# GpSimd takes the plain LayerNorm normalisations, the ternary weights and an output bias from VectorE in a two-layer gated cross-attention kernel

## The chip, the cores and the metric

The kernel runs on one core of one Trainium2 chip. The time is that of one execution on the device, in microseconds, and lower is better. Engines are named as the profile names them: PE is TensorE (PEld its weight loads), DVE is VectorE, ACT is ScalarE, POOL is GpSimd, SP is SyncE. PSUM is the memory into which PE writes; SBUF is the working memory from which all engines read.

## What is computed

A residual stream `x` of two batches of 512 tokens and 128 channels passes through two layers. Each layer is a cross-attention and a feed-forward net, and each of them is added back through a tanh gate.

```python
# layer 0
x = x + tanh(g_xattn[0]) * (attention(ln(x), ctx) @ Wo + bo)       # 16 heads, 77 context rows
h = ln(x)
gate = silu(bitlinear(h, w_gate)); up = bitlinear(h, w_up)
x = x + tanh(g_ffn[0]) * bitlinear(gate * up, w_down)
# bitlinear: activations rounded to 8 bits per token, weights to -1, 0, 1
#   scale = 1 / clip(mean(|w|), 1e-5);     wq = clip(round(w * scale), -1, 1) / scale
#   scale = 127 / clip(max(|x|), 1e-5);    xq = clip(round(x * scale), -128, 127) / scale
# layer 1
a = ln(x) * ln1_g + ln1_b                     # then self-attention a1 (masked after the softmax) + GELU net
a = ln(a) * ln2_g + ln2_b                     # then cross-attention a2 on ctx + GELU net
x = x + gate * a
x = x + gate * (softmax router) * expert_7(ln(x))
```

`ln` subtracts the mean of a token's 128 channels and divides by the root of the variance plus 1e-5.

## The kernel before

Tokens lie on the 128 partitions: a batch `b` (0 or 1) is four tiles `t` of 128 tokens by 128 channels, so a tensor such as `xn[:, b, t, :]` is one 128x128 tile. Each engine has its own program, written out by hand in order, and the programs meet at semaphores. An engine works its program in that order: an instruction that waits holds all behind it on the same engine.

The stages, with the time that they take in the profile: loading, folding the layer-0 projections into one key matrix and the first LayerNorm (0 to 23 us); the layer-0 cross-attention, 16 units `i` (23 to 84 us); the quantised feed-forward net, eight token tiles `n` (84 to 115 us); the LayerNorms and first projections of self-attention a1 (115 to 140 us); a1's 32 heads (140 to 280 us); its output and GELU net `a1f` (280 to 320 us); the cross-attention a2, again 16 units (323 to 377 us); the GELU nets `a2f` and `f1` (377 to 420 us).

**A LayerNorm** is done for one batch in these steps. DVE takes statistics (`ln_stats`, four L1167 and four L1170) and writes `var` (L1175). POOL raises it to the power -0.5 (`power`, L842) into `rstd`. DVE normalises (`ln_norm`): for a plain site four `tensor_scalar` of one tile each, `(src - mean) * rstd`, into `xn` (L1182); for the sites with gain and bias (`ln1`, `ln2`) four instructions with the gain (L1187) and four with `rstd` and the bias (L1191) into `x1`. DVE waits for `rstd` before the first of either, and behind `ln_norm` waits until it is complete. Then PE transposes `xn` (L397), ACT copies the result to `xnT` (L918, L921), and PE goes on with matmuls. Sites are called after what they feed: `x`, `f0`, `ln1`, `a1`, `a1f`, `ln2`, `a2`, `a2f`, `f1`.

**A unit of cross-attention** (`cross`, for `l0` and `a2`): PE scores (L470), DVE row maxima `nmx` (L1248), ACT eight exponentials (L988), DVE reciprocal sums `rden` (L1253), POOL multiplies the 128x616 probabilities by them (L851), PE transposes them (L397), DVE copies the transposes out of PSUM (L1260), PE multiplies by the values (L490). PE's program for step `i` is scores of `i`, values of `i-3`, transposes of `i-2`. Other work hangs in this loop by its step: on DVE `ternary` at steps 6, 8 and 10 of `l0` (three instructions on a 128x512 matrix, L1234, L1236, L1238), the output bias at steps 9 and 11 (L1304), LayerNorm `f0` of batch 0 at steps 13 to 15, and in `a2` at steps 0 to 2 the two LayerNorms `ln2` and `a2` of batch 1, at steps 13 and 14 `a2f` of batch 0. POOL computes `rstd` of `f0` behind its multiplication 12, of `a2` behind 0, of `a2f` behind 12.

**The quantised net**, per tile `n`: PE two matmuls (L564), ACT silu (L1035), DVE product with the second matmul (L1402), DVE the largest magnitude (L1411), its clip (L1408), reciprocal (L1414) and times 127 (L1416), ACT multiply and round by adding a large constant (L1050), DVE clip to -128..127 (L1421, waits for ACT's rounding of tile `n-2`), ACT to bf16 (L1058), PE transposes (L585), DVE copy (L1429), PE matmul (L596). The input of the net is rounded the same way: `scale_x`, `round_x` on ACT, `clip_x` on DVE (L1358), `x_to_bf16` on ACT.

At the start, DVE's program is: context statistics, statistics of `x`, normalisation of `x` for both batches, then `ctxn` (L1387), which waits for `crstd` from POOL (L864), and then its share of the copies of the folded keys out of three PSUM banks (L1210, `fold("l0", 0)`), which PE's fold matmuls (L438) need free.

## Time and profile before

| | |
|---|---|
| Time before, median of 3 runs | 426.03 us (424.16 to 428.45) |
| The profiled execution's own time | 422.04 us |
| its span, first to last instruction | 420.3 us |
| PE busy | 344.0 us, 82% of the span, 2037 instructions |
| PEld busy | 235.8 us, 56% |
| DVE busy | 315.2 us, 75%, 748 instructions |
| ACT busy | 279.4 us, 66% |
| POOL busy | 107.6 us, 26%, 206 instructions |
| Chain that ended last | PE 43%, DVE 13%, issue 7%, ACT 7%, POOL 1% |

Busy time is the time in which an engine has an instruction in work. Matmuls are pipelined, so a busy PE need not be at its peak. The clock of PE is granted in two levels, 1.2 GHz (0.5 in the profile) and 2.4 GHz (1.0). The chain that ended last is followed back from the last instruction to what released each step; in this trace it reaches back to 120 us only.

### The profile page before, as it was taken

The numbers are of one execution on the slowest core, as the hardware profiler recorded it, in microseconds if no ns is written. First come the engines' busy times: TensorE is split into PE (matmuls) and PEld (weight loads), VectorE is DVE, ScalarE is ACT, GpSimd is POOL, SyncE is SP. The second block draws the span as 40 slices with busy tenths as digits, with TensorE's granted clock in tenths as the row PEclk, the third lists the DMA queues.
The fourth block names the chain that finished last, engine by engine and source line by source line (L and its number), as shares of the span: only waits on it lengthen the run. The fifth ranks groups of instructions, "written<-read, shape, count | busy, mean of one in ns | idle before, by whom it ended". The sixth has DMA issues, their size and how long they took to land.

```text
span 420.3 us, 6805 instructions
## 1 busy us (share of the span) xinstructions
PE 344.0 (82%) x2037; PEld 235.8 (56%) x2038; DVE 315.2 (75%) x748; ACT 279.4 (66%) x965; POOL 107.6 (26%) x206
## 2 busy tenths in 40 slices
PE   4978999726437888998989988978998799977796
PEld 4756877602312444555545545566676588864656
DVE  3656789688885688899899998975757876855515
ACT  4465888657413787888889888853825899855051
POOL 5311344300010122232222222232101444520100
PEclk9999999966558999999999999999999899999989
DMA  7920000000003653861790494000000000000001
GB/s 222 346 100 2 2 1 2 1 0 1 2 0 82 158 136 89 200 140 26 168 207 3 101 205 96 0 4 0 2 0 2 1 2 0 2 0 2 0 0 51
DMA packets 8860, 24.75 MB, mean 59 GB/s; under 512 B 2667, under 2 KB 2744, under 8 KB 8568
## 3 DMA queue, kind: packets, MB, share of 16 engines
q1 hardware_dynamic: 8824, 24.32, 22.9%
q8 instruction: 17, 0.28, 0.3%
q14 instruction: 19, 0.16, 0.1%
HBM read 7.00 MB, written 0.52 MB: 18 GB/s over the span
## 4 chain that ended last, share of the span: by engine, by line
PE 43%; DVE 13%; issue 7%; ACT 7%; POOL 1%; DVEq 0%
PE ps L397 9%; PE ps L537 5%; PE ps L521 5%; DVE nm L1513 4%; PE ps L615 4%; PE ps L667 4%; PE ps L490 4%; PE ps L630 4%; ACT pring L1111 3%; PE ps L470 3%; PE ps L438 2%; DVE arena L1485 2%; PE ps L701 2%; DVE xn L1182 1%; PE ps L683 1%
## 5 line engine op out<-in xcount | busy, mean ns | idle before, releaser
L1111 ACT ACTIVATE pring<-ps,nm 128x512 f32<-128x512 f32 x128 | 87.0, 688 | 12.7 <-DVE nm L1513 9.6
L988 ACT ACTIVATE arena<-ps,nmx 128x77 f32<-128x77 f32 x256 | 79.1, 344 | 14.1 <-DVE nmx L1248 13.6
L1513 DVE TENSOR_REDUCE nm<-ps 128x2 f32<-128x1024 f32 x64 | 78.0, 1220 | 6.1 <-PE ps L630 5.9
L875 POOL TENSOR_SCALAR_AFFINE_SELECT pring<-pring 128x128 f32<-128x128 f32 x128 | 38.8, 303 | 109.5 <-ACT pring L1111 109.5
L630 PE MATMUL ps<-Ks,Qs 128*128 128x512 f32 x128 | 52.6, 463 | 8.6 <-ACT pring L1111 6.2
L397 PEld LDWEIGHTS ps<-ident,pring 128*128 128x128 f32 x352 | 39.4, 140 | 32.7 <-issue 17.8
L397 PE MATMUL ps<-ident,pring 128*128 128x128 f32 x352 | 52.1, 277 | 6.7 <-ACT xn L1078 2.8
L988 ACT ACTIVATION_READ_ACCUMULATOR arena<-ps,nmx 128x1 f32 x256 | 57.3, 224 | 0.0
L851 POOL TENSOR_TENSOR arena<-arena,rden 128x616 f32<-128x616 f32 x32 | 39.2, 1226 | 63.1 <-DVE rden L1253 63.1
L490 PE MATMUL ps<-arena 128*128 128x128 f32 x320 | 42.4, 280 | 6.3 <-DVE arena L1260 6.3
L490 PEld LDWEIGHTS ps<-arena 128*128 128x128 f32 x320 | 38.6, 192 | 15.5 <-DVE arena L1260 14.9
L1485 DVE COPY arena<-ps 128x384 f32<-128x384 f32 x64 | 39.5, 617 | 7.7 <-PE ps L397 7.5
L842 POOL TENSOR_TENSOR rstd<-var,minus_half 128x4 f32<-128x4 f32 x18 | 18.2, 1010 | 105.3 <-DVE var L1175 105.2
L470 PE MATMUL ps<-arena,xnT 128*128 128x320 f32 x128 | 41.0, 445 | 3.3 <-ACT arena L988 1.7
L1260 DVE COPY arena<-ps 128x384 f32<-128x384 f32 x64 | 27.9, 477 | 10.4 <-PE ps L397 10.4
L630 PEld LDWEIGHTS ps<-Ks,Qs 128*128 128x128 f32 x128 | 21.3, 190 | 25.0 <-ACT pring L1111 14.1
L1248 DVE TENSOR_REDUCE nmx<-ps 128x8 f32<-128x616 f32 x32 | 25.5, 798 | 9.9 <-PE ps L470 9.6
L397 PE MATMUL ps<-ident,arena 128*128 128x128 f32 x200 | 29.3, 279 | 2.9 <-POOL arena L851 1.1
L470 PEld LDWEIGHTS ps<-arena,xnT 128*128 128x128 f32 x128 | 22.4, 195 | 10.1 <-ACT arena L988 2.7
L397 PEld LDWEIGHTS ps<-ident,arena 128*128 128x128 f32 x200 | 23.2, 143 | 5.5 <-issue 1.6
L1111 ACT ACTIVATION_READ_ACCUMULATOR pring<-ps,nm 128x1 f32 x128 | 25.8, 202 | 0.0
L1015 ACT ACTIVATE hid<-ps,cols_sb 128x512 f32<-128x512 f32 x24 | 16.1, 688 | 12.5 <-PE ps L521 12.4
(147 smaller groups left out, 539.4 us busy)
## 6 DMA issues: line engine op xcount, KB each, us to landing
Qs<-qh SPq DMA_DIRECT2D x24, 128.0 KB, 2.4
Qs<-ql SPq DMA_DIRECT2D x24, 128.0 KB, 2.4
Ks<-xo SPq DMA_DIRECT2D x24, 128.0 KB, 2.4
Ks<-xb SPq DMA_DIRECT2D x24, 128.0 KB, 2.4
wa_sb<-in_wa SPq DMA_DIRECT2D x1, 1536.0 KB, 15.2
early<-in_w SPq DMA_DIRECT2D x2, 512.0 KB, 8.2
wa_sb<-in_wa SPq DMA_DIRECT2D x1, 1024.0 KB, 17.4
Qs<-hid SPq DMA_DIRECT2D x16, 64.0 KB, 2.0
```

Of the source, the lines that this page charges most:

```text
L397: m = pe.transpose(bank(res)[0:width, t * parts:(t + 1) * parts], src(t), ident[0:parts, 0:parts])
L470: m = pe.matmul(bank(res)[:, 0:4 * HS], xnT[:, b, t * P:(t + 1) * P], FK[:, b, c0:c0 + 4 * HS], start=True, stop=True)
L490: m = pe.matmul(bank(res)[:, t * P:(t + 1) * P], PTc[:, j % 4, k, :], VO[:, b, half * (NCH // 2) + k, :], start=(half == 0 and k == 0), st ...
L630: filled(pe.matmul(bank(f"S{i}"), Qs[:, j, b, i * P:(i + 1) * P], Ks[:, j, b, :], start=True, stop=True), ("s1", n, i))
L851: pool.tensor_tensor(pv, pv, rden[:, j % 4, :].unsqueeze(2).to_broadcast([P, 8, M]), ALU.mult).then_inc(pn_ready, 1)
L875: pool.affine_select(out=blk, in_=blk, compare_op=ALU.is_gt, fill=0.0, base=0, pattern=[[1, P]], channel_multiplier=-1).then_inc(masked, 1)
L988: ins = act.activation(Pc[:, i % PC_SLOTS, h * HS:h * HS + M], bank(where[key])[:, h % 4 * HS:h % 4 * HS + M], ACT.Exp, bias=nmx[:, i % 4, ...
L1111: release(act.activation(pring[:, n % 2, i, :], bank(f"S{i}"), ACT.Exp, bias=nm1[:, n % 8, i:i + 1], accum_out=den1[:, n % 8, i:i + 1]), ( ...
L1248: dve.tensor_reduce(nmx[:, i % 4, :].rearrange("p (q h) -> p q h", q=2), src, AX.X, ALU.max, negate=True).then_inc(nmax_ready, 1)
L1260: release(dve.tensor_copy(PTc[:, j % 4, k0:k1, :].rearrange("p k n -> p (k n)"), bank(res)[:, 0:(k1 - k0) * P]), key)
L1485: release(dve.tensor_copy(dst, src), key)
L1513: dve.tensor_reduce(nm1[:, n % 8, 2 * u:2 * u + 2], pair(u), AX.X, ALU.max, negate=True).then_inc(nm1_ready, 1)
```

## The change

1. `normalise_tokens`, new, on POOL: behind `rstd` of each plain site POOL itself writes `xn`, four `tensor_scalar` of one 128x128 tile each. `ln_norm` is gone from DVE. `xn_ready` counts the plain sites alone.
2. `ternary` and the output bias move to POOL: one step behind each of its multiplications 1 to 12 of `l0`. The bias is now `bo * gate` once (128x128) and then one 128x512 addition per batch.
3. POOL's powers move inside `cross`: `f0` batch 0 from behind multiplication 12 to behind 13, `a2` batch 1 from 0 to 4. PE's transposes and ACT's copy of `a2` batch 1 move from step 3 to step 6.
4. The sites with gain and bias stay on DVE: `ln_gain` no longer waits for `rstd`, only `ln_bias` does. For `ln2` batch 1 they are spread over steps 0 to 3 of `a2` and its statistics go to step 4.
5. The clips of rounded activations (L1358, L1421) are left out: a value scaled by 127 over its token's largest magnitude rounds to at most 127. The constant 1/127 is folded into the clip of the maximum, so that the multiplication by 127 (L1354, L1416) goes too, and `dout` takes one instruction instead of two.
6. Before `a1f`, POOL also waits for `RT_ready` and `OT_ready`, since `xn` holds other data during the heads.

```diff
@@ gpsimd
+            def normalise_tokens(site, b):
+                src = {"x": r, "f0": r, "a1": x1, "a1f": xo, "a2": x1, "a2f": xo, "f1": r}[site]
+                pool.wait_ge(rstd_ready, nth(site, b))
+                for t in range(NT):
+                    ins = pool.tensor_scalar(xn[:, b, t, :], src[:, b, t, :], mv[:, b, t, 0:1],
+                                             rstd[:, b, t:t + 1], ALU.subtract, ALU.mult)
+                ins.then_inc(xn_ready, 1)
@@ power
                             .then_inc(rstd_ready, 1)
+                        if site not in LN_AFFINE:
+                            normalise_tokens(site, b)
@@ gpsimd cross
-                    if site == "l0" and j == 12:
+                    if site == "l0" and 1 <= j < 4:
+                        output_bias(j - 1)
+                    if site == "l0" and 4 <= j < 13:
+                        ternary((j - 4) // 3, (j - 4) % 3)
+                    if site == "l0" and j == 13:
                         power("f0", batches=[0])
-                    if site == "a2" and j == 0:
+                    if site == "a2" and j == 4:
                         power("a2", batches=[1])
@@ tensor cross
-                    if site == "a2" and i == 3:
+                    if site == "a2" and i == 6:
                         ln_transposes("a2", 1)
@@ vector
-            def ln_norm(site, b, src, affine=None, dst=None):
+            def ln_gain(site, b, src, tiles=range(NT)):
+                for t in tiles:
+                    did(dve.scalar_tensor_tensor(x1[:, b, t, :], src[:, b, t, :], mv[:, b, t, 0:1],
+                                                 row(site + "_g"), ALU.subtract, ALU.mult))
+
+            def ln_bias(site, b, tiles=range(NT)):
+                settle()
                 dve.wait_ge(rstd_ready, nth(site, b))
@@ vector, quantised net
                 if 1 <= n <= NB * NT:
-                    did(dve.reciprocal(hinv[:, bj, tj:tj + 1], hmx[:, bj, tj:tj + 1]))
-                    settle()
-                    dve.tensor_scalar(hinv[:, bj, tj:tj + 1], hinv[:, bj, tj:tj + 1], 127.0, None, ALU.mult)\
-                        .then_inc(hscale_ready, 1)
-                if 2 <= n < NB * NT + 2:
-                    j = n - 2
-                    dve.wait_ge(hround_ready, j + 1)
-                    dve.tensor_scalar(h_in[:, j % 4, :], h_in[:, j % 4, :], MAGIC + 127.0, MAGIC - 128.0,
-                                      ALU.min, ALU.max).then_inc(hclip_ready, 1)
+                    dve.reciprocal(hinv[:, bj, tj:tj + 1], hmx[:, bj, tj:tj + 1]).then_inc(hscale_ready, 1)
@@ vector
             ln_stats("a1", 0, x1)
             f0_out(1)
-            ln_norm("a1", 0, x1)
             ln_stats("ln1", 1, r)
```

POOL at the start of the program, in the kernel before (`crstd` is the factor of the context's LayerNorm, `arena` holds folded keys and their zero pads):

```order
L842 TENSOR_TENSOR rstd<-var,minus_half 128x4 [waits var_ready] x2
L864 TENSOR_TENSOR crstd<-cvar,minus_half 77x2 [waits cvar_ready]
L830 MEMSET arena 128x16x3 x4
L835 MEMSET arena 128x8x3 [waits full_T1]
L835 MEMSET arena 128x8x3 x2
```

The same place in the changed kernel:

```order
L889 TENSOR_TENSOR rstd<-var,minus_half 128x4 [waits var_ready]
L850 TENSOR_SCALAR xn<-r,mv,rstd 128x128 [waits rstd_ready]
L850 TENSOR_SCALAR xn<-r,mv,rstd 128x128 x3
L889 TENSOR_TENSOR rstd<-var,minus_half 128x4 [waits var_ready]
L850 TENSOR_SCALAR xn<-r,mv,rstd 128x128 [waits rstd_ready]
L850 TENSOR_SCALAR xn<-r,mv,rstd 128x128 x3
L917 TENSOR_TENSOR crstd<-cvar,minus_half 77x2 [waits cvar_ready]
L838 MEMSET arena 128x16x3 x4
```

Eight normalising instructions now stand ahead of `crstd` and of the zeroed pads.

DVE in the quantised net, one tile, in the kernel before (`hid` holds the products and their roundings, `hmx` and `hinv` the largest magnitude and its inverse):

```order
L1402 SCALAR_TENSOR_TENSOR hid<-ps,du,hid 128x512 [waits silu_ready,full_S3]
L1408 TENSOR_SCALAR hmx<-hmx 128x1
L1411 TENSOR_REDUCE hmx<-hid 128x1 [waits free_S3,dve_step]
L1414 RECIPROCAL hinv<-hmx 128x1
L1416 TENSOR_SCALAR hinv<-hinv 128x1 [waits dve_step]
L1421 TENSOR_SCALAR hid<-hid 128x512 [waits hround_ready]
L1429 COPY hid<-ps 128x512 [waits full_T0]
```

The same tile in the changed kernel:

```order
L1416 SCALAR_TENSOR_TENSOR hid<-ps,du,hid 128x512 [waits silu_ready,full_S3]
L1421 TENSOR_SCALAR hmx<-hmx 128x1 [waits dve_step]
L1425 TENSOR_REDUCE hmx<-hid 128x1 [waits free_S3,dve_step]
L1428 RECIPROCAL hinv<-hmx 128x1
L1435 COPY hid<-ps 128x512 [waits full_T0]
```

Two of seven instructions are gone, and with the clip the wait for ACT's rounding.

## Rows read from the trace of the kernel before

**Rows 1.** Busy time by stretch, all engines: length; PE, PEld, DVE, ACT, POOL; clock, DMA
```profile
78.00:110.00 32.00, 15.90 (x103) 9.23 (x103) 25.54 (x85) 20.86 (x43) 2.23 (x2) 0.70 0.00 1
140.00:280.00 140.00, 122.07 (x759) 71.12 (x758) 126.47 (x163) 118.64 (x309) 39.25 (x129) 1.00 0.50 113
```

**Rows 2.** Timeline of 12 to 19 us: start, length, engine, instruction, idle before
```profile
12.91 1.02 POOL L842 TENSOR_TENSOR rstd<-var,minus_half 128x4 f32<-128x4 f32 x1 [6.77 <-DVE var L1175]
15.31 0.78 POOL L864 TENSOR_TENSOR crstd<-cvar,minus_half 77x2 f32<-77x2 f32 x1
17.05 0.53 DVE L1210 TENSOR_SCALAR arena<-ps 128x154 f32<-128x154 f32 x2
18.68 0.55 DVE L1210 TENSOR_SCALAR arena<-ps 128x154 f32<-128x154 f32 x2 [1.10 <-PE ps L438]
```

**Rows 3.** Timeline in the first attention, POOL and PE
```profile
55.04 1.24 PE L470 MATMUL ps<-arena,xnT 128*128 128x320 f32 x4
55.27 1.22 POOL L851 TENSOR_TENSOR arena<-arena,rden 128x616 f32<-128x616 f32 x1 [1.50 <-DVE rden L1253]
...
57.80 1.24 PE L470 MATMUL ps<-arena,xnT 128*128 128x320 f32 x4
61.08 1.24 PE L470 MATMUL ps<-arena,xnT 128*128 128x320 f32 x4
```

**Rows 4.** Timeline of the quantised net: table load ahead of it, one tile on DVE
```profile
83.59 1.28 ACT L910 ACT_TABLE_LOAD   x1
...
98.60 0.74 DVE L1402 SCALAR_TENSOR_TENSOR hid<-ps,du,hid 128x512 f32<-128x512 f32 x1
...
100.05 0.15 DVE L1414 RECIPROCAL hinv<-hmx 128x1 f32<-128x1 f32 x1
100.31 0.42 DVE L1421 TENSOR_SCALAR hid<-hid 128x512 f32<-128x512 f32 x1
100.64 0.42 DVE L1429 COPY hid<-ps 128x512 bf16<-128x512 bf16 x1
100.97 0.74 DVE L1402 SCALAR_TENSOR_TENSOR hid<-ps,du,hid 128x512 f32<-128x512 f32 x1
```

**Rows 5.** Timeline of 114 to 133 us, first LayerNorms of layer 1
```profile
114.91 1.14 DVE L1187 SCALAR_TENSOR_TENSOR x<-r,mv,rows_sb 128x128 f32<-128x128 f32 x4 [0.76 <-POOL rstd L842]
...
121.66 1.09 PE L397 MATMUL ps<-ident,xn 128*128 128x128 f32 x4 [6.85 <-DVE xn L1182]
...
130.23 1.01 POOL L842 TENSOR_TENSOR rstd<-var,minus_half 128x4 f32<-128x4 f32 x1 [6.10 <-DVE var L1175]
...
132.63 1.11 DVE L1182 TENSOR_SCALAR xn<-x,mv,rstd 128x128 f32<-128x128 f32 x4
```

**Rows 6.** Groups of instructions on POOL, shapes apart: busy us, mean ns, idle
```profile
L875 POOL TENSOR_SCALAR_AFFINE_SELECT pring<-pring 128x128 f32<-128x128 f32 x128 | 38.8, 303 | 109.5 <-ACT pring L1111 109.5
L842 POOL TENSOR_TENSOR rstd<-var,minus_half 128x4 f32<-128x4 f32 x18 | 18.2, 1010 | 105.3 <-DVE var L1175 105.2
```

**Rows 7.** Timeline, DVE and POOL where both read SBUF
```profile
55.89 0.88 DVE L1234 TENSOR_SCALAR pring<-pring,winv 128x512 f32<-128x512 f32 x1
...
214.78 0.43 DVE L1493 COPY xn<-rd 128x512 f32<-128x512 f32 x1
214.87 0.49 POOL L875 TENSOR_SCALAR_AFFINE_SELECT pring<-pring 128x128 f32<-128x128 f32 x1 [0.63 <-ACT pring L1111]
```

**Rows 8.** Timeline in the second attention, from its start to steady state
```profile
327.86 0.80 DVE L1248 TENSOR_REDUCE nmx<-ps 128x8 f32<-128x616 f32 x1
...
333.68 0.80 DVE L1248 TENSOR_REDUCE nmx<-ps 128x8 f32<-128x616 f32 x1
...
359.80 1.23 POOL L851 TENSOR_TENSOR arena<-arena,rden 128x616 f32<-128x616 f32 x1 [1.53 <-DVE rden L1253]
...
362.43 0.71 PE L397 MATMUL ps<-ident,arena 128*128 128x128 f32 x5
```

**Rows 9.** Timeline at 380 us, LayerNorm before the second plain FFN
```profile
380.54 1.12 DVE L1182 TENSOR_SCALAR xn<-xo,mv,rstd 128x128 f32<-128x128 f32 x4 [1.12 <-POOL rstd L842]
```

More of the change, by code:

```diff
@@ L71 @@
             ("f1", 0), ("f1", 1)]
+LN_AFFINE = ("ln1", "ln2")
+LN_PLAIN = [(site, b) for site, b in LN_ORDER if site not in LN_AFFINE]
 LN_TRANSPOSED = [(site, b) for site, b in LN_ORDER if site not in ("f0", "ln1", "ln2")]
@@ L882, in _ @@
             zero_diag(1)
+            pool.wait_ge(RT_ready, NSTEP)
             power("a1f", batches=[0])
@@ L1227, in mean_weights @@
                 settle()
[L1228 to L1238 removed]
+                dve.reciprocal(winv[:, :], wmean[:, :]).then_inc(winv_ready, 1)
             def cross(site):
@@ L1266, in cross @@
                         ln_stats("a2f", 0, xo)
-                    if site == "a2" and i == 14:
-                        ln_norm("a2f", 0, xo)
                     if site == "l0" and i == 12:
@@ L1317, in ln_both @@
             def ln_both(site, before, src):
-                before(0)
-                ln_stats(site, 0, src)
-                before(1)
-                ln_norm(site, 0, src)
-                ln_stats(site, 1, src)
-                ln_norm(site, 1, src)
+                for b in range(NB):
+                    before(b)
+                    ln_stats(site, b, src)
             def bias_and_residual(name):
@@ L1383, in _ @@
             dve.wait_ge(loaded["x"], 16)
-            ln("x", r)
+            for b in range(NB):
+                ln_stats("x", b, r)
             dve.wait_ge(crstd_ready, 1)
@@ L1551, in _ @@
             ln_stats("a2f", 1, xo)
-            ln_norm("a2f", 1, xo)
             bias_and_residual("a2_li3_b")
```

148 lines of the change are left out of this document (67 added, 81 removed).

## The prediction, made before the changed kernel ran

> **What bounds the kernel now.** I read the busy time by stretch first, then the timeline of each place where the change touches a program. In a1's heads (140 to 280 us) DVE is busy 126.5 of 140 us, PE 122.1, and the change touches nothing there [rows 1]: a third of the time is out of reach, and POOL's masks, DVE's maxima and copies stay as they are. From 78 to 110 us DVE is busy 25.5 of 32 us and PE 15.9, at a clock of 0.70: here DVE sets the pace [rows 1]. In the first attention PE's unit starts lie 2.76 us apart where nothing holds it (55.04 to 57.80), but 3.28 where DVE has a ternary step late (57.80 to 61.08), and PE works without a gap in the first of the two [rows 3]: there, and in the second attention, which has the same loop, DVE work is hidden except where it is bunched. So what DVE gives away is worth little in the two attentions and much from 84 to 135 us.
>
> **The price of the moved work.** No POOL instruction of before is a `tensor_scalar` with two per-token scalars. Nearest is the mask, one 128x128 tile in and out: 0.303 us [rows 6]. Four of them make 1.21 us; with 0.1 for their wait I take N = 1.3 us for a batch's normalisation, against 1.11 on DVE [rows 5]. Bounds: below, 1.0, since unwaited POOL instructions overlap a little. Above, from the powers: 1.01 us for four columns [rows 6], 0.78 for two [rows 2], a line that meets nothing at 0.55 us of start; with it a tile costs 0.6 and N is 2.4. I stay near the mask, which has the same shape and does no power.
>
> **Terms, in order of time** (minus is a gain):
>
> 1. Start. `crstd` ended at 15.31 + 0.78 = 16.09 [rows 2]. Now both normalisations stand ahead of it: first power until 13.93, N, power 1.01, N, 0.78, and 0.1 for each of four waits: 18.7. DVE's first copy out of the fold banks, at 17.05 [rows 2], waits for it through `ctxn` and comes at 19.25, 2.2 later. Part is covered: a later copy waited 1.10 for PE [rows 2], so PE had not yet asked for every bank. I take +1.4; without cover it is +2.2.
> 2. Units of the first attention. Of eleven spacings three are longer than 2.76: by 0.52 as shown [rows 3], by as much again at the third ternary step, and by 0.13. Sum -1.2. On POOL each step goes into the 1.50 us idle before a multiplication [rows 3]: a 128x512 step costs at most four masks, 1.2 us, and is hidden; if it took 2 us or more, the transposes would wait.
> 3. End of the first attention. POOL now does power and N behind multiplication 13, some 2.4 us where 1.5 are idle; what DVE gives back there POOL takes. 0, from -0.4 to +0.6.
> 4. Head of the quantised net: `x_to_bf16` and the table load of silu no longer wait for `clip_x`, which DVE did behind its last copies. The load ended at 83.59 + 1.28 = 84.87 [rows 4] and held up ACT's copy of the transposes, which follow PE's last values by 0.4 and need no load. -0.7, an estimate; at least 0.
> 5. Tiles. A tile takes 100.97 - 98.60 = 2.37 us. From the reciprocal at 100.05 to the copy at 100.64 there are 0.59 us, for the multiplication and the clip [rows 4]; 0.1 remains, so 1.9 us a tile, -0.45 with ACT's three instructions a tile as the next limit. With the first tiles (`clip_x` of batch 1 held up PE's transposes) and the two trailing clips this is the same as seven tiles: -3.1.
> 6. `ln1` batch 0: the gain waited 0.76 us for POOL [rows 5]: -0.7.
> 7. `a1` batch 1 decides when the heads begin. Before, its power began at 130.23 and ended at 131.24, but DVE normalised only at 132.63, since copies of values stood ahead, until 133.74 [rows 5]. POOL needs 131.24 + 0.1 + 1.3 = 132.6: -1.1. For batch 0 PE's transposes waited 6.85 us until 121.66 for DVE, which did the output of the net in between [rows 5]; POOL does not, and comes some 0.3 earlier, within this term.
> 8. `a1f` +0.2 and `a2` batch 0 +0.1: N is 0.2 longer than on DVE, covered for `a1f` by PE's other work.
> 9. Start of the second attention: the maxima at 327.86 and 333.68 were late behind DVE's LayerNorms [rows 8], and ACT with its exponentials, then PE, waited for each. -1.2.
> 10. Step 6 of `a2`: PE transposes `a2` batch 1 right behind the probabilities of unit 4. A multiplication ends at 359.80 + 1.23 = 361.03, PE's transposes of it begin at 362.43 [rows 8] and take 0.6. So PE asks 2.0 us behind the end of the multiplication; power and N need 2.5. +0.5. The next multiplication comes some 1.1 late, inside the 1.4 just named.
> 11. `a2f` batch 1: DVE normalised at 380.54 behind a wait of 1.12, and nothing covered it [rows 9]; N is +0.1 net of one hand-over. But DVE now goes straight on to six additions, most of them with two inputs from SBUF, which run beside POOL: +0.8 (next part).
> 12. `f1`: POOL needs not wait for DVE's addition of the other batch. -0.5.
>
> Sum: 1.4 - 1.2 + 0 - 0.7 - 3.1 - 0.7 - 1.1 + 0.3 - 1.2 + 0.5 + 0.9 - 0.5 = -5.4. The profiled execution took 422.04 us and would take 416.6. The runs shown have a median 4.0 above it; I take the same difference from the median: 426.03 - 5.4 = 420.6, in round numbers 420.5.
>
> **Two engines at one memory.** DVE's ternary step at 55.89 took 0.88 us; POOL's multiplication had begun at 55.27 and ended at 56.49 [rows 7, 3], and DVE ended at 56.77. The other way round, POOL's mask at 214.87 took 0.49 instead of 0.30 while DVE's copy ran from 214.78 to 215.21 [rows 7, 6]. So each waits for the other, whoever came first. A POOL tile beside a row of 0.69 us DVE additions can wait up to 0.69 each time, 2.8 us for four. I put 0.8 into term 11, since the first additions are over when POOL begins, and 0.2 into term 8.
>
> The Trainium skill has this as a rule: SBUF — State Buffer, Who interferes with whom, says that DVE and GpSimd share one pair of ports as an exclusive lock, which a DVE instruction in a two-port mode takes, or one with two SBUF inputs against a GpSimd instruction that reads SBUF. The trace agrees in both directions. By that rule in full, terms 8 and 11 would be +5.6 instead of +1.2. Its GPSIMD Engine Reference, Engine selection, calls one-input work on GpSimd roughly line-rate and two-input work about half as fast as on VectorE; the first would put N near 1.3, the mask row says as much.
>
> **Rivals.**
>
> - *Slower: a POOL tile is dear.* N enters the end about nine times per microsecond: twice at the start, once each at `f0` batch 1, `a1` batch 1, `a2` batch 0, step 6, `a2f` batch 0 and 1, `f1`. Gain is gone at N = 1.3 + 5.4/9 = 1.9 (0.48 us a tile), and 1% slower begins at 2.4 (0.6 a tile), the upper bound above. At 0.65 a tile it is -5.4 + 9 x 1.3 = +6.3: 432 us. For it: the power row shows that a POOL instruction can have a large fixed part. Against: the mask of the same shape. 0.12.
> - *Same: the lock.* If the four tiles each wait a full DVE addition at `a1f` and `a2f` batch 1, +2.6 and +1.3 (PE's other work covers the rest), less 1.0 already counted: -2.5 in all, 423.5 us. For it: rows 7. 0.20.
> - *Same: another limit in the quantised net.* ACT has three instructions a tile and PE runs at the low clock for part of it. If a tile stays at 2.2 us, term 5 is -1.2 and the sum -3.5: 422.5 us. For it: PE's clock of 0.70 [rows 1]. 0.11.
> - *Faster still: PE's clock.* The clock of 0.70 from 78 to 110 us [rows 1] is the low level in most of the net, after waits. With shorter waits the high level may come back earlier. At 1.00 PE's 15.9 busy us there would be 11.1; were half of the 4.8 on the path, it is -2.4 to -3: 417.5 us. 0.10.
> - Forecast as above: 0.47.
>
> **How the numbers follow.** 1% of 426 is 4.3 us, about what a measurement of this kernel can tell from no change. Faster by more: forecast and clock, 0.57. Within: lock and net, 0.31. Slower: the dear tile, 0.12. The range goes from 415 (clock case, with the lower bound of N, 9 x 0.3 = 2.7 less) to 427 (N of 2.0 in the forecast); beyond lie the rest of the dear tile above and little below. The forecast's own range is 417 to 424.
>
> **What the profile of the changed kernel would show.** POOL: xn<-r of 128x128 at 0.30 to 0.35 us each; 0.6 proves the first rival. Start: the copies of folded keys begin at about 19.2, and PE's first scores 1.4 later than before. Tiles: DVE's products 1.9 us apart; 2.2 is the third rival. Heads: their first maximum 5.4 us earlier than before, which is the whole gain; if it is less than 3 earlier, the forecast is wrong. From there to 320 us the difference stays the same within 0.5. In `a2` a wait of PE for POOL's `xn` at step 6. At `a2f` batch 1 POOL's four tiles longer than 0.35 beside DVE's additions. POOL's normalisation of `f0` batch 1 over 1 us late, or multiplications that PE waits for in each unit, would make it wrong.

## The result, and the profile after

The changed kernel took 452.65 us (median of 4 runs, 452.0 to 453.46), beside 425.1 us for the kernel before in the same comparison (4 runs, 422.21 to 428.45): a ratio of 1.0646, 95% interval 1.0563 to 1.073. It is 27.5 us slower. The forecast was 420.5 us with a range that ended at 427. A few executions are slower at a lower granted clock; the medians given are of all of them, and the ratios leave these out.

| | before | after |
|---|---|---|
| time of the profiled execution | 422.04 us | 453.46 us |
| span | 420.3 us | 451.7 us |
| mean granted clock of PE | 0.943 | 0.906 |

The first page to read is the one on which the forecast had staked most. POOL's groups of instructions after, shapes apart (busy us, mean ns, idle before):

```profile
L850 POOL TENSOR_SCALAR xn<-r,mv,rstd 128x128 f32<-128x128 f32 x24 | 18.7, 793 | 0.6
L850 POOL TENSOR_SCALAR xn<-xo,mv,rstd 128x128 f32<-128x128 f32 x16 | 14.5, 919 | 0.4
```

A tile takes 0.79 us and not the 0.30 of the mask [rows 6]. A batch's four take 3.12 to 3.18 us; with the wait of 0.1 between power and tiles N, the cost of a normalisation, is 3.26 us, where the forecast had 1.3 and an upper bound of 2.4. The tiles that read `xo` are dearer still, 0.92 us in the mean; among them are those of `a2f` batch 1, which run beside DVE's additions. The waits of PE for POOL's normalisations (in total, times, longest):

```profile
PE ps L405 <- POOL xn L850: 25.1, 7, 7.7
```

In the kernel before, PE's waits for DVE's normalisations came to 12.2 us, in four.

The start, in the timeline (start, length, engine, instruction, idle before), answers to [rows 2]:

```profile
21.67 0.53 DVE L1401 TENSOR_SCALAR ctxn<-ctx_sb,cmv,crstd 77x64 f32<-77x64 f32 x2 [7.88 <-POOL crstd L917]
22.12 0.99 DVE L1258 TENSOR_SCALAR arena<-ps 128x154 f32<-128x154 f32 x4
...
22.80 4.78 PE L446 MATMUL ps<-arena,early 128*128 128x308 f32 x10 [4.29 <-DVE arena L1258]
```

The first copy out of the fold banks comes at 22.12 us, and had come at 17.05. The end of the first attention, POOL and PE, where [rows 3] is the undisturbed rhythm:

```profile
77.99 1.22 POOL L900 TENSOR_TENSOR arena<-arena,rden 128x616 f32<-128x616 f32 x1 [0.64 <-DVE rden L1291]
79.17 1.03 POOL L889 TENSOR_TENSOR rstd<-var,minus_half 128x4 f32<-128x4 f32 x1
80.33 3.13 POOL L850 TENSOR_SCALAR xn<-r,mv,rstd 128x128 f32<-128x128 f32 x4
83.42 1.22 POOL L900 TENSOR_TENSOR arena<-arena,rden 128x616 f32<-128x616 f32 x1
...
81.48 1.38 PE L498 MATMUL ps<-arena 128*128 128x128 f32 x10 [0.83 <-DVE arena L1298]
84.79 1.30 PE L405 MATMUL ps<-ident,arena 128*128 128x128 f32 x5 [1.93 <-POOL arena L900]
86.71 2.50 PE L498 MATMUL ps<-arena 128*128 128x128 f32 x10 [0.62 <-DVE arena L1298]
```

Multiplication 14 waits behind the normalisation, PE stands for 1.93 us, and then the same ten matmuls take 2.50 us instead of 1.38: PE's granted clock is 1.00 from 81.48 to 82.86 us and 0.50 from 84.79 to 89.20, that is, 2.4 and then 1.2 GHz. The gap comes back as a second loss. The same happens at the second batch of `a2f`, which answers to [rows 9]; POOL, then PE:

```profile
402.97 1.40 POOL L889 TENSOR_TENSOR rstd<-var,minus_half 128x4 f32<-128x4 f32 x1 [9.38 <-DVE var L1230]
404.48 4.45 POOL L850 TENSOR_SCALAR xn<-xo,mv,rstd 128x128 f32<-128x128 f32 x4
...
409.07 1.09 PE L405 MATMUL ps<-ident,xn 128*128 128x128 f32 x4 [5.07 <-POOL xn L850]
411.02 6.08 PE L529 MATMUL ps<-xnT,wa_sb 128*128 128x512 f32 x8 [0.87 <-ACT xnT L973]
```

The same place before:

```profile
381.80 0.63 PE L397 MATMUL ps<-ident,xn 128*128 128x128 f32 x4 [1.27 <-DVE xn L1182]
...
383.30 3.70 PE L521 MATMUL ps<-xnT,wa_sb 128*128 128x512 f32 x8 [0.87 <-ACT xnT L918]
```

The part that did most nearly what it should is the quantised net: one tile of it follows the other in 1.98 us on average (106.38 to 114.30 for four), where [rows 4] had 2.37:

```profile
98.00:128.00 30.00, 13.32 (x78) 7.41 (x78) 23.56 (x83) 15.46 (x28) 5.33 (x7) 0.50 0.00 1
```

(DVE 23.56 busy of 30 us and PE at 0.50, the low clock, throughout; columns as in [rows 1].) The first and the last of these five products on DVE:

```profile
106.38 0.75 DVE L1416 SCALAR_TENSOR_TENSOR hid<-ps,du,hid 128x512 f32<-128x512 f32 x1 [1.42 <-ACT hid L1090]
...
114.30 0.74 DVE L1416 SCALAR_TENSOR_TENSOR hid<-ps,du,hid 128x512 f32<-128x512 f32 x1
```

### Where the time went, stretch by stretch

POOL's powers and its multiplications by 1/denominator mark the same points of the program in every kernel. The table gives the length of each stretch before, and how much longer (+) or shorter (-) it is elsewhere, from the timelines of POOL. The columns are explained with the experiments: N is the cost of one normalisation on POOL; "apart" is N = 1.2 with DVE's additions kept out of the way; "DVE" has all normalisations back on DVE.

| stretch | before | forecast | after, N 3.3 | N 2.2 | N 1.2 | N 1.2, apart | DVE | clips only |
|---|---|---|---|---|---|---|---|---|
| start to multiplication 0 | 28.1 | +1.4 | +6.1 | +3.8 | -0.3 | -0.4 | -0.1 | -0.7 |
| to multiplication 11 of `l0` | 39.3 | -1.2 | -1.8 | -1.8 | -1.8 | -1.8 | -1.8 | 0.0 |
| to the power of `f0` batch 1 | 19.2 | 0 | +5.2 | +1.3 | +0.2 | +0.2 | +3.0 | 0.0 |
| to the power of `ln1` batch 0 | 27.3 | -3.8 | -1.6 | -2.6 | -3.8 | -3.7 | -3.9 | -3.4 |
| to the power of `a2` batch 0 | 205.4 | -1.6 | +5.1 | +2.1 | -1.6 | -1.8 | -1.5 | -1.1 |
| to the last multiplication of `a2` | 52.9 | -0.6 | +7.2 | +1.2 | +0.3 | +0.2 | +0.4 | +0.2 |
| to the power of `f1` batch 0 | 20.9 | +0.9 | +9.9 | +7.6 | +5.6 | +1.1 | 0.0 | 0.0 |
| to the end | 27.2 | -0.5 | +1.3 | -1.5 | -2.5 | -2.6 | 0.0 | 0.0 |
| sum | 420.3 | -5.4 | +31.4 | +9.9 | -3.9 | -8.7 | -3.9 | -5.0 |

The first row carries some chance: DVE begins on x between 9.8 and 11.3 us in these runs. Each column is one execution. In the columns N 2.2, N 1.2 and "apart" the kernels don't compute the whole normalisation; they measure a price and could not be used.

### The profile page after: what moved, and what is told of

The parts are those of the page before. It is cut to its first block, busy times and chain, and to the rows that moved or that the text cites. A ratio compares the mean times of both kernels' runs of the same rounds, so it can differ in the third digit from the quotient of the medians.

```text
span 451.7 us, 6788 instructions
## 1 busy us (share of the span) xinstructions
PE 361.7 (80%) x2037; PEld 246.4 (55%) x2038; DVE 288.8 (64%) x659; ACT 279.5 (62%) x965; POOL 165.0 (37%) x274
## 4 chain that ended last, share of the span: by engine, by line
PE 38%; DVE 13%; POOL 9%; issue 7%; ACT 5%; DMA 1%; SPq 1%; DVEq 0%; ACTq 0%; POOLq 0%
PE ps L405 8%; POOL xn L850 6%; PE ps L529 4%; PE ps L623 4%; PE ps L675 4%; PE ps L498 4%; DVE nm L1513 3%; PE ps L638 3%; PE ps L545 3%; PE ps L478 3%; ACT pring L1166 2%; POOL rstd L889 2%; PE ps L709 2%; PE ps L446 2%; DVE stats L1222 2%
## 5 line engine op out<-in xcount | busy, mean ns | idle before, releaser
L498 PE MATMUL ps<-arena 128*128 128x128 f32 x320 | 45.9, 294 | 4.3 <-DVE arena L1298 4.3
L498 PEld LDWEIGHTS ps<-arena 128*128 128x128 f32 x320 | 41.8, 205 | 13.8 <-DVE arena L1298 13.3
L478 PE MATMUL ps<-arena,xnT 128*128 128x320 f32 x128 | 43.8, 470 | 1.8 <-ACT xnT L973 1.1
L1298 DVE COPY arena<-ps 128x384 f32<-128x384 f32 x64 | 28.1, 482 | 20.3 <-PE ps L405 20.1
L405 PE MATMUL ps<-ident,arena 128*128 128x128 f32 x200 | 30.4, 285 | 7.2 <-POOL arena L900 5.4
L405 PE MATMUL ps<-ident,xn 128*128 128x128 f32 x80 | 14.0, 306 | 25.8 <-POOL xn L850 25.1
L478 PEld LDWEIGHTS ps<-arena,xnT 128*128 128x128 f32 x128 | 23.7, 206 | 10.0 <-issue 3.5
L973 ACT ACTIVATE xnT<-ps,cols_sb 128x512 f32<-128x512 f32 x8 | 6.2, 777 | 36.0 <-PE ps L405 36.0
```

Source lines behind the costliest of these rows:

```text
L405: m = pe.transpose(bank(res)[0:width, t * parts:(t + 1) * parts], src(t), ident[0:parts, 0:parts])
L478: m = pe.matmul(bank(res)[:, 0:4 * HS], xnT[:, b, t * P:(t + 1) * P], FK[:, b, c0:c0 + 4 * HS], start=True, stop=True)
L498: m = pe.matmul(bank(res)[:, t * P:(t + 1) * P], PTc[:, j % 4, k, :], VO[:, b, half * (NCH // 2) + k, :], start=(half == 0 and k == 0), st ...
L1298: release(dve.tensor_copy(PTc[:, j % 4, k0:k1, :].rearrange("p k n -> p (k n)"), bank(res)[:, 0:(k1 - k0) * P]), key)
```

## Experiments

### Undo the normalisations

```
 power():  no normalise_tokens
+ln_norm(site, b, src) on DVE for x, f0, a1, a1f, a2, a2f, f1, where the kernel before has it
 (a2 batch 1 behind unit 5); ternary, bias, ln2 spread, clips as in the changed kernel
```

> One part of the change is undone: the plain normalisations are DVE's again, at the places where the kernel before has them (batch 1 of a2 behind unit 5, since its steps are moved). All else is the changed kernel: POOL keeps the ternary steps and the bias, ln2 is spread, the clips are gone. Price theory (the 27.5 us of loss come from POOL's normalisation of 3.1 us a batch in place of 1.3, at nine places, and from PE's clock that falls behind the longer waits): what is left are the terms of the forecast that don't hang on it, -1.2 (units), -0.7 (head of the net), -3.1 (tiles), -0.7 (ln1) and about half of -1.2 (second attention): -6.3, so 418.8 us beside 425.1 for the kernel before, a ratio near 0.985; first copy out of the fold banks again at 17.1 us and the heads' first maximum at about 135. Rival, the other moved work (POOL's ternary steps of up to 1.5 us, two multiplications late, or the later a2 batch 1) costs too: 425 to 435 us. Rival, the trace's shift through the first attention (+6.05 at 34 us, +6.2 at 85) already shows that the unit term is 0: then 420 us.

Measured: 419.58 us, ratio 0.9895 (0.9834 to 0.9956). So POOL's normalisations are the whole loss: with them back on DVE the rest of the change is 1% faster. The units up to multiplication 11 did gain 1.8 us, so the rival "unit term is 0" falls: the changed kernel's shift was +6.05 us at the first multiplication of the attention and +6.2 at the last because what the units gained had been lost again by its end. But 3.0 us go at the end of the first attention. There the power, which had stood behind multiplication 12, stands behind 13. DVE waits for it, and PE for DVE:

```profile
69.70 1.49 POOL L868 TENSOR_SCALAR wf0b<-pring 128x512 bf16<-128x512 f32 x1
71.83 1.23 POOL L898 TENSOR_TENSOR arena<-arena,rden 128x616 f32<-128x616 f32 x1 [0.64 <-DVE rden L1296]
...
74.08 1.12 DVE L1246 TENSOR_SCALAR xn<-r,mv,rstd 128x128 f32<-128x128 f32 x4 [1.58 <-POOL rstd L889]
...
76.82 2.35 PE L498 MATMUL ps<-arena 128*128 128x128 f32 x10 [2.34 <-DVE arena L1303]
```

The ternary step of 1.49 us ahead of multiplication 13 does not hold it: POOL stands idle for 0.64 us behind that step, until DVE's `rden`. DVE's `var` is there at 71.21 us, when POOL is free; but the multiplication comes first, and the power begins only at 73.01. No run moves the power alone; the last kernel below puts it back behind 12 and packs the ternary steps as well, and has +0.6 in this stretch.

### One wide instruction instead of four

```
-for t in range(NT):
-    pool.tensor_scalar(xn[:, b, t, :], src[:, b, t, :], mv[:, b, t, 0:1], rstd[:, b, t:t + 1], ...)
+pool.tensor_scalar(xn[:, b, :, :], src[:, b, :, :], mv[:, b, 0, 0:1], rstd[:, b, 0:1], ...)
```

> The changed kernel, but POOL normalises a batch in one instruction of 128x512 with the mean and the factor of its first tile for all four tiles. This changes what is computed (three quarters of the tokens get another tile's mean and factor); no time depends on the values. If a POOL instruction with two per-token scalars costs by its start and hardly by its columns (one scalar: 0.61 us for 128 columns, 0.69 for 512, in the trace of after), it takes 0.87 us and N is 0.97 instead of 3.13. Price theory: the sum of the forecast holds once N is what it assumed, -5.4 - 9 x 0.3 = -8.1: 417 us, or 418.5 with a unit term of 0; PE's clock comes back with it. Rival, the loss is the hand-over to POOL and the shared memory rather than the tile's price: over 435 us. Rival, cost by columns: one instruction of 3 us, and the time stays at 450.

Measured: 432.98 us, ratio 1.0195 (1.0121 to 1.0268). The kernel uses the first tile's mean and factor for all four tiles. The instruction took 2.08 us and not 0.87, so the expectation's price was wrong and so was its 417 us; the rival's 3 us was wrong too:

```profile
L849 POOL TENSOR_SCALAR xn<-r,mv,rstd 128x512 f32<-128x512 f32 x6 | 12.5, 2076 | 0.7
```

It is a dose all the same. N went from 3.26 to 2.17, by 1.09 us, and the time by 4.5% or 19 us: 17.6 us for each us of N, twice the nine that the forecast worked with.

### What a POOL instruction costs, by its form

```
 power("f1")
+pool.wait_ge(out_ready, NB)
+19 forms of instruction, each alone and waited for, twice; then eight normalising tiles
+at a time, alone and beside DVE instructions of 128x256, 16 of each of three forms
```

> The changed kernel with 38 further POOL instructions behind its outputs, each alone and waited for, and then eight POOL tiles at a time (two per-token scalars, 128x128) alone and beside three kinds of DVE instructions of 128x256 in SBUF. The whole takes some 80 us longer than the changed kernel; only the duration of each instruction counts. Form theory: columns are cheap on POOL and the start is dear, by form: two per-token scalars 0.79 us at 128 columns, 0.72 at 16 and 0.87 at 512; one scalar 0.61; immediates 0.53; the mask 0.30 since it is another kind of instruction. Rival, columns count: 16 columns take under 0.4 us and 512 over 2. Output in bf16: 1.49 us at 512 columns against 0.69 in float32, if it is the type; the same, if it was something else in that step. Lock: a POOL tile takes 0.79 us alone and up to 0.4 more beside DVE instructions with two SBUF inputs; beside DVE's one-input product too if it runs in a fast mode.

The timeline of POOL behind the outputs (the two passes agree to 0.01 us):

```profile
464.96 0.44 POOL L961 TENSOR_SCALAR pring<-pring,mv,rstd 128x16 f32<-128x16 f32 x1
465.50 0.79 POOL L962 TENSOR_SCALAR pring<-pring,mv,rstd 128x128 f32<-128x128 f32 x1
466.39 1.22 POOL L963 TENSOR_SCALAR pring<-pring,mv,rstd 128x256 f32<-128x256 f32 x1
467.71 2.07 POOL L964 TENSOR_SCALAR pring<-pring,mv,rstd 128x512 f32<-128x512 f32 x1
469.88 0.45 POOL L965 TENSOR_SCALAR pring<-pring,rstd,mv 128x128 f32<-128x128 f32 x1
470.43 0.61 POOL L966 TENSOR_SCALAR pring<-pring,rstd 128x128 f32<-128x128 f32 x1
471.12 0.30 POOL L967 TENSOR_SCALAR pring<-pring 128x128 f32<-128x128 f32 x1
471.51 0.53 POOL L968 TENSOR_SCALAR pring<-pring 128x128 f32<-128x128 f32 x1
...
472.45 1.49 POOL L970 TENSOR_SCALAR pring<-pring 128x512 f32<-128x512 f32 x1
474.02 1.49 POOL L971 TENSOR_SCALAR wf0b<-pring 128x512 bf16<-128x512 f32 x1
```

L961 to L964 are the tile's form, subtract and multiply by per-token values, at 16, 128, 256 and 512 columns: nearly a line, some 0.38 us of start and 3.3 ns a column. L965 is the same width with **multiply first and add second**: 0.45. L966 is one multiplication by a per-token value: 0.61, dearer than the multiplication with an addition. L967 is multiply and add by constants: 0.30; L968 the constant multiplication alone: 0.53. L970 and L971 are that one at 512 columns, in float32 and in bf16: 1.49 both. So the form theory, in which columns are cheap, fell, and the rival came near (0.44 and 2.07 us for its under 0.4 and over 2). Columns do count, and the output type doesn't. The price also depends on which operations the instruction has. Multiply-and-add is cheap (the ternary's first step, at 512 columns with one per-token value, took 0.69 in the changed kernel), and so is min-and-max (0.61 at 512). Subtract-and-multiply and the single operations tried, a multiplication and a subtraction, are 1.4 to 1.8 times as dear at 128 columns and over twice at 512. The mask at 128 columns took 0.29 here.

Eight tiles alone took 6.23 us, 0.78 each. Beside DVE additions of two SBUF inputs they took 7.63, and DVE's sixteen additions took 7.15 instead of 6.32 alone. Both engines pay. The other two forms didn't meet a set of eight each, since DVE went on without a stop. The third set ran beside both of them:

```profile
500.02 4.63 DVE L1657 TENSOR_SCALAR xb<-xb 128x256 f32<-128x256 f32 x16
500.61 8.58 POOL L985 TENSOR_SCALAR xn<-x,mv,rstd 128x128 f32<-128x128 f32 x8 [0.17 <-POOL xn L985]
504.75 7.72 DVE L1659 SCALAR_TENSOR_TENSOR xb<-xb,mv,x 128x256 f32<-128x256 f32 x16
```

Its fifth tile began at 504.77 us. So four tiles took 4.16 us beside the one-input product (1.04 each) and four took 4.42 beside the product-and-addition (1.10). In the fourth set, 6.88 us, DVE was done after about four tiles. All three forms slow POOL; which slows it most, these runs don't tell.

### The clips alone, on the kernel before

```
-clip_x(0), clip_x(1), the clip of each tile; factors 127 and 1/127 as steps of their own
+the factors folded into the steps ahead; ACT waits for the rounding itself
```

> The kernel before with one part of the change alone: both rounding clips left out and the factors of 127 folded into the steps ahead of them. Forecast terms 4 and 5: -0.7 at the head of the net and -3.1 over its tiles (2.37 us a tile becomes 1.9): 421.3 us beside 425.1, ratio 0.991. Rival, another limit (ACT's three instructions a tile, or PE at its low clock) holds a tile at 2.2 us: 423.2 us, ratio 0.9955. Rival, the gain is given back at f0's end, where PE waits for the next thing anyway: 425.

Measured: 417.72 us, ratio 0.9874 (0.9807 to 0.9942). This part alone is faster than the whole set with DVE's normalisations (0.9895), though the intervals overlap. By the table -3.4 us fall in the net (forecast -3.8) and -1.1 in the stretch behind it. Of these, 0.9 fall between the last power ahead of the heads and the first behind them, where no edit touches anything. The -0.7 at the start is chance. ACT's three instructions did not become the limit at 2.2 us: the third rival falls.

### POOL tiles at the price that the forecast had

```
-pool.tensor_scalar(xn.., src.., mean, rstd, ALU.subtract, ALU.mult)
+pool.tensor_scalar(xn.., src.., 1.0, 0.0, ALU.mult, ALU.add)
```

> The changed kernel, but each POOL tile of the plain normalisation multiplies by 1 and adds 0 as constants: 0.30 us alone in the probe's run, where mean and factor cost 0.79. The normalisation's arithmetic is left out; waits, order, sizes and writes stay. This gives the sum of the forecast its own N: 4 x 0.30 + 0.1 = 1.3 us. Theory that only the price of the tile was wrong: -5.4, so 419.5 beside the 423 to 426 of the kernel before, ratio 0.987. From the run with one instruction of 2.07 us a batch (a loss of 1.95%, 8.3 us) to here N falls by 0.87 us; by the forecast's nine places that is 7.8 us less, so about 0: 424; by the slope between that run and the changed kernel (6.46% to 1.95%, 19 us for 1.05 us of N, 18 places) it is 16 us less: 416. Rival, the hand-over to POOL and the shared memory cost by themselves: it stays above 428.

Measured: 418.67 us, ratio 0.99 (0.9832 to 0.9968). The kernel leaves out the normalisation's arithmetic and keeps its instructions. N is 1.17 here. The sum of the forecast was -5.4, the trace gives -3.9, and three of its eight stretches are hit within 0.3 us and two more within 1. The run with all normalisations on DVE has -3.9 too: even at this price moving them gains nothing by itself. The start and the end are 1.7 and 2.0 us better than said, and the stretch with the second batch of `a2f` is 4.7 worse (+5.6 for +0.9). From here to N = 2.17 is 3.0% or 12.5 us, so the slope is 12.5 us for each us of N below 2.2 and 17.6 above. The intervals of the ratios leave room for one slope; the spans of the traces give 13.8 and 19.7. Between the two runs, by a straight line, the break-even lies near N = 1.5, an estimate, where the prediction had 1.9.

### The same normalisation in the cheaper form

```
+dve.tensor_scalar(nmean, mean, -1.0, None, ALU.mult)            (ahead of var)
+pool.tensor_tensor(nmr, nmean, rstd, ALU.mult)                  128x4
-pool.tensor_scalar(xn.., src.., mean, rstd, ALU.subtract, ALU.mult)
+pool.tensor_scalar(xn.., src.., rstd, nmr, ALU.mult, ALU.add)
```

> The changed kernel with the same normalisation written in another form: POOL works out minus mean times factor for the four tiles first (128x4) and each tile is then x * factor + that, multiplication first and addition second, 0.45 us a tile in the probe's run in place of 0.79. DVE has one more instruction of 0.17 us at each LayerNorm and a wait behind it, POOL one of about 0.3. N is 0.3 + 0.1 + 4 x 0.45 + 0.1 = 2.3. Form theory: tiles at 0.45 inside the kernel too, and the time lies a little over that of the run with N of 2.17: ratio 1.025 to 1.04. Rival, the probe's price doesn't hold beside DVE: tiles over 0.6 us and a ratio over 1.045.

Measured: 436.5 us, ratio 1.0306 (1.0223 to 1.039), the same computation as the changed kernel's and shorter by 3.4% of the time before. The probe's price holds where nothing runs beside it, and less where DVE does:

```profile
L854 POOL TENSOR_SCALAR xn<-r,rstd,nmr 128x128 f32<-128x128 f32 x24 | 10.4, 447 | 0.6
L854 POOL TENSOR_SCALAR xn<-xo,rstd,nmr 128x128 f32<-128x128 f32 x16 | 8.5, 544 | 0.4
```

Of 0.79 us a tile, 0.34 was the choice and order of its two operations. N is 2.10 here, a little less than with the wide instruction, yet the span is 5.4 us longer (435.6 and 430.2). So N alone doesn't fix the time. This kernel has one more instruction on DVE and on POOL in each LayerNorm; what the 5.4 us are was not looked into.

### Filling PE's waits

```
 claim(pe, res, ("ln", site, b), ...)
+for _ in range(9 to 48, by place):
+    pe.transpose(bank(res)[0:P, 0:P], ident, ident)
 pe.wait_ge(xn_ready, ...)
```

> The changed kernel with extra work for PE: in front of seven of its waits for POOL's xn it transposes the identity 9 to 48 times into the bank that it fills next (0.142 us each at the high clock), as much as fills each wait as the changed kernel has it (2.6, 7.7, 1.6, 1.8, 3.0, 5.1 and 3.4 us). It removes nothing of what it waits for. Clock theory: PE's clock falls because PE stood idle, and the matmuls behind the waits then take twice as long (L529 6.08 us at a2f batch 1 for the 3.70 of before); filled, they run at the high clock, and 4 to 8 us come back: 445 to 449, ratio 1.047 to 1.055, mean clock over 0.93 for 0.906. Rival, the fall has another cause: 453 or more (the filling itself may overrun a wait by some tenths), L529 still at 6.0.

Measured: 446.18 us, ratio 1.0543 (1.0473 to 1.0614); mean clock 0.930 for 0.906. PE did more work, and the kernel was 4.4 us faster by the ratios, whose intervals overlap, and 6.6 us by the spans. At `a1` batch 0, where the changed kernel's PE waited 7.7 us:

```profile
122.72 7.53 PE L414 MATMUL ps<-ident 128*128 128x128 f32 x48
130.51 0.66 PE L405 MATMUL ps<-ident,xn 128*128 128x128 f32 x4 [0.26 <-POOL xn L853]
132.03 1.13 PE L626 MATMUL ps<-xnT,wa_sb 128*128 128x512 f32 x2 [0.87 <-ACT xnT L976]
```

In the changed kernel the two matmuls behind took 2.07 us. So there the fall of the clock follows PE's idleness. At `a2f` batch 1 the fillers ended early, 1.48 us of idle time stayed, and the eight matmuls took 5.38 us, better than 6.08 and far from 3.70; the detail of the expectation that they would be fast was wrong. So the length of the last wait doesn't by itself say what the matmuls behind it will take.

### The context's power first

```
 zero_diag(1)
+crstd <- pow(cvar)
 power("x")
-crstd <- pow(cvar)
```

> The changed kernel with one wait moved: the power for the context (crstd) stands ahead of the two powers and normalisations of x on POOL, and not behind them. Theory, the start's loss of 6.0 us is this one queue: crstd ends before the LayerNorm of x begins, DVE's copies out of the fold banks begin at about 14 us, right behind its statistics, PE no longer stands for 4.29 us, and the first multiplication comes at 28 us or earlier instead of 34.1; the two normalisations of 3.1 us then end at about 21 and PE asks for xn at about 21: no wait over 1 us. Rival, PE waits for xn instead: the first multiplication comes at 30 or later.

One run: 445.11 us, and multiplication 0 at 27.56 us instead of 34.13:

```profile
6.23 0.72 POOL L916 TENSOR_TENSOR crstd<-cvar,minus_half 77x2 f32<-77x2 f32 x1
...
17.88 3.12 POOL L850 TENSOR_SCALAR xn<-r,mv,rstd 128x128 f32<-128x128 f32 x4
...
20.87 1.04 PE L405 MATMUL ps<-ident,xn 128*128 128x128 f32 x8
```

POOL's two normalisations of 3.1 us then cost PE nothing, as it comes to `xn` just when they end. The loss of 6.1 us at the start was one small instruction that stood behind them.

### DVE's additions kept out of the way

```
 ln_stats("a2f", 1, xo)
+dve.wait_ge(xn_ready, nthN("a2f", 1))
 bias_and_residual("a2_li3_b")          (the same at a1f)
```

> The changed kernel with its own POOL tiles of 0.79 us; DVE does its additions for a1f and a2f only behind POOL's normalisation of batch 1. At a2f batch 1 the changed kernel has the power in 1.40 us, the four tiles in 4.45 and a wait of PE of 5.07 us. Lock theory: 1.01 and 3.12, PE's wait 3.3 us, so 1.7 us less in the step from a2f's power to f1's (20.25 us, becomes 18.5), and about 0.9 less at a1f. PE's eight matmuls behind it stay at 6.0, as the wait is still over 3 us. Rival: the tiles slow down by each other and not by DVE; 4.4 us again.

> The run with tiles of 0.30 us once more (multiplies by 1, adds 0, the normalisation's arithmetic left out), and DVE now does its additions for a1f and a2f only behind POOL's normalisation of batch 1. In the run without this, at a2f batch 1 the power took 1.38 us and the four tiles 2.71, where they take 1.01 and 1.21 alone, PE waited 3.29 us for them, and its eight matmuls behind took 5.70 instead of 3.70. Lock theory: power and tiles go back to 1.01 and 1.21, PE's wait becomes 1.4 us, about what it is in the kernel before (1.27), and the eight matmuls take 3.70 again, since the clock doesn't fall in so short a wait: the step from a2f's power to f1's, 18.07 us in that run and 13.60 before, becomes 13.7 to 14, and the whole 3 to 4 us shorter, 415 us, ratio 0.98. Rival, DVE's additions are now late for something: no gain, the final product waits for them. Rival on the clock, the fall comes with any wait for POOL: still 5.7 for the eight.

On the changed kernel (one run, 450.84 us) the power went from 1.40 to 1.03 us and the tiles from 4.45 to 3.13, PE's wait from 5.07 to 3.38, the eight matmuls from 6.08 to 5.40; the step from this power to that of `f1` from 20.25 to 17.41 us, where 18.5 was expected, because the clock came back sooner. At `a1f` nothing changed, where 0.9 was expected: PE has other work there.

The same edit on the kernel with tiles of 0.30 us gives the clearest pair of the study. First the run of N = 1.2 as it was, POOL then PE:

```profile
373.64 1.38 POOL L888 TENSOR_TENSOR rstd<-var,minus_half 128x4 f32<-128x4 f32 x1 [7.17 <-DVE var L1229]
375.11 2.71 POOL L850 TENSOR_SCALAR xn<-xo 128x128 f32<-128x128 f32 x4
...
377.96 1.09 PE L405 MATMUL ps<-ident,xn 128*128 128x128 f32 x4 [3.29 <-POOL xn L850]
379.91 5.70 PE L529 MATMUL ps<-xnT,wa_sb 128*128 128x512 f32 x8 [0.87 <-ACT xnT L972]
```

and with the additions behind the wait:

```profile
373.32 1.01 POOL L888 TENSOR_TENSOR rstd<-var,minus_half 128x4 f32<-128x4 f32 x1 [7.17 <-DVE var L1229]
374.42 1.09 POOL L850 TENSOR_SCALAR xn<-xo 128x128 f32<-128x128 f32 x4
...
375.65 0.63 PE L405 MATMUL ps<-ident,xn 128*128 128x128 f32 x4 [1.29 <-POOL xn L850]
377.15 3.70 PE L529 MATMUL ps<-xnT,wa_sb 128*128 128x512 f32 x8 [0.87 <-ACT xnT L972]
```

It took 412.87 us, ratio 0.976 (0.9665 to 0.9855), with the normalisation's arithmetic left out as before. Working beside DVE's additions cost POOL 2.0 us. PE's wait was longer by as much, its granted clock behind it was 0.50 from 378 to 384 us, where with the additions apart it was 1.00 throughout, and its transposes and matmuls took another 2.5: 4.4 us from a price that was entered as 0.8.

### What the runs recommend

```
 clips out, factors folded; all normalisations and the order of ln2 and a2 as before
 POOL: output_bias at j = 1..3
+      ternary(q, 0), ternary(q, 1) at j = 4, 6, 8; ternary(q, 2) at j = 5, 7, 9
+      power("f0", batch 0) at j = 12
```

> What the runs so far recommend: clips left out and factors folded (ratio 0.987 alone), ternary steps and output bias on POOL but packed into the units 4 to 9 so that none of 1.49 us stands ahead of f0's power, all normalisations on DVE, and the order of ln2 and a2 as in the kernel before. In the run with DVE's normalisations the units up to multiplication 11 had gained 2.0 us, and 1.6 of it went back at unit 13, where a ternary step and the power stood ahead of each other and PE waited 2.34 us and came back at the low clock; and step 6 of a2 cost 1.6. Expected: -3.7 (clips) - 1.9 (units) = -5.6 against the kernel before by the trace, plus whatever of DVE's start is jitter: 418 to 419 by that, and at least as good as the clips alone; ratio 0.98 to 0.988. Rival: units gained in the first attention only move the idle time to its end: the same as the clips alone.

Measured: 416.82 us (6 runs, 416.29 to 417.85), ratio 0.985 (0.9799 to 0.9902): faster than both kernels. Its trace has -1.8 us in the units of the first attention, gives 0.6 back at its end, -3.9 in the net and -1.2 behind it. Whether it beats the clips alone (0.9874) can't be told by the times; by the traces it does so by 0.8 us in the span, and by 2.0 from multiplication 0 on.

## Why the prediction was wrong

**The step that failed** is the price of the moved work. N was taken from the mask, "which has the same shape and does no power", and bounded above by a line through the powers. The probe shows that the mask is among the cheapest POOL instructions at this width (0.29) and the subtract-and-multiply the dearest measured, 0.79 us; the bound of 0.6 a tile was no bound, since start and columns were both taken from other kinds. The first rival had the mechanism and a check ("0.6 proves the first rival"), and by that check the trace decides for it; but it had 0.12, and its 432 us were for 0.65 a tile. (Its break-even of N = 1.9 is 0.45 a tile and not 0.48, with the forecast's own wait of 0.1.)

**The multiplier failed as well.** Nine us for each us of N was too little in both doses, 12.5 from N = 1.2 to 2.2 and 17.6 from there to 3.3. By nine, 9 x 1.96 = 17.6 us would have been the difference from the forecast, which was 33 us (+27.5 for -5.5). Two causes are shown. Cover is finite: term 3 was entered at 0, as an even exchange between POOL and DVE, which holds at N = 1.2 (+0.2 at the end of the first attention) and not at 3.3 (+5.2). And the long waits are paid twice, since PE comes back at 1.2 GHz: behind the wait of 5.07 us at `a2f` the matmuls took 2.4 us more, behind one of 1.29 nothing more, and the filled waits gave 4 to 7 us back. It isn't so everywhere: at `f1` the matmuls took 5.40 us in both kernels, behind 2.14 us before and 3.37 after. How much of the rest belongs to each isn't separated.

**The terms at their own N** are judged by the run with cheap tiles.

- Term 1, +1.4: N = 1.2 had -0.3 with x 1.5 us earlier, so something from -0.3 to +1.2; right in mechanism, and the wait of `ctxn` for `crstd` was the whole of the +6.1 after.
- Term 2, -1.2: right. The eleven spacings of PE's scores sum to 31.56 us before and to 30.36 with N = 1.2. POOL's multiplications, by which the table goes, have -1.8 at number 11, but -1.4 at number 12 and -1.3 at number 13. The step of 1.49 us is dearer than the 1.2 given and still hidden.
- Term 3, 0: +0.2 by the table and -0.3 counted from multiplication 13, but +3.0 in the run with DVE's normalisations: the power behind multiplication 13 was on the path of DVE, which the forecast didn't look at.
- Terms 4 and 5, -3.8: -3.8. A tile 1.98 us for the 1.9 said. In the changed kernel N at `f0` batch 1 took 2.2 of it back.
- Terms 6 to 8 up to `a2`, -1.6: -1.6, but by luck. The heads' first maximum came at 130.88 us for 140.24, 9.4 earlier and not 5.4, and from there to the first power of `a1f` 3.3 us were lost. Some 1.1 of them are the waits that point 6 of the change puts ahead of that power; another 1.9 were lost between 146 and 163 us, where the granted clock (0.91 from 140 to 160) was below the 1.00 of the kernel before. The kernel with the clips alone gained 1.1 in this stretch without any of the three terms.
- Terms 9 and 10 with `a2` batch 0, -0.6: +0.3. In the run with DVE's normalisations, counted from the power of `a2` batch 0, the start of the second attention was 1.5 us ahead at multiplication 3 and 0.4 behind at multiplication 5. So the later step gave back 1.9 even with DVE normalising; PE waited 0.83 us for `xn` there. The rest wasn't tested by itself.
- Term 11, +0.9: +5.6, and +1.1 once the additions are out of the way. The mechanism was named, and a size too ("2.8 us for four"), but then 0.8 was taken, with the argument that the first additions would be over. They were not: power and tiles took 2.0 us longer, and PE's clock, which the term left out, added 2.5. The Trainium skill has the rule on who shares the ports (SBUF — State Buffer, Who interferes with whom); by the forecast's own reckoning it would have cost 2.8 us at each of `a1f` and `a2f`. At `a2f` the trace agrees in kind, with 2.0 us; that the stretch came to +5.6 is not that rule's 5.6. At `a1f` additions kept apart changed nothing.
- Term 12, -0.5: -2.5 at N = 1.2. PE waited 1.29 us for `xn` there instead of 2.14, so the term itself was 0.85. The rest is again PE's clock, since the eight matmuls behind took 3.70 us, and before:

```profile
396.29 0.63 PE L397 MATMUL ps<-ident,xn 128*128 128x128 f32 x4 [2.14 <-DVE xn L1182]
...
397.60 5.40 PE L521 MATMUL ps<-xnT,wf_sb 128*128 128x512 f32 x8 [0.69 <-ACT xnT L921]
```

The rival on PE's clock thus had a mechanism that the runs show, but not its place: in the quantised net the granted clock was 0.58 before and 0.62 with N = 1.2.

The Trainium skill's GPSIMD Engine Reference, Engine selection, calls one-input work on GpSimd roughly line-rate. The runs don't bear that out as a rule of price: 0.79 us for a tile for which DVE needs 0.28 (1.11 for four), and 0.30 for another one-input form of the same size. The forecast had used the sentence as support for the mask's price.

Of the checks named, "first maximum 5.4 us earlier; if it is less than 3 earlier, the forecast is wrong" was the useful one: in the changed kernel it came 10.05 us later (150.29). The words behind it, that this was "the whole gain", failed even with cheap tiles, as term 6 shows.

## What to carry to other kernels

Price an instruction that moves to POOL by a row of the same operations, not only of the same shape; where there is none, let the range reach several times the nearest row, and find the break-even before the sum. Count a price's multiplier at both ends of its range: cover that hid 1.2 us on a queue here didn't hide 3.3, and a wait of PE that grew from 1.3 to 3.3 us cost its length and again the clock. What a slow POOL step holds up can be a small instruction behind it: one power moved ahead of two normalisations gave 6.6 us back at the first multiplication.
